# A two-layer recurrent and windowed-attention kernel: the second feed-forward product from rounded parts and rests, one convolution tap on ScalarE

## What is computed

```python
def _layer(x, wqkv, qs, ksc, wo, lg, lb, w1, b1, w2, b2):
    h = shift_token(x)
    ...                                  # q, k, v, rotary, local attention
    x = x + o @ wo
    h = shift_token(x)
    h = (h - mu) / jnp.sqrt(var + 1e-05) * lg + lb
    h = h @ w1 + b1
    a, g = jnp.split(h, 2, axis=-1)
    h = a * jax.nn.gelu(g, approximate=False)
    x = x + h @ w2 + b2
...
x_conv = _causal_depthwise_conv(x, conv_w, conv_b)   # four taps
r_t = jax.nn.sigmoid(x_conv @ W_r.T + b_r)
i_t = jax.nn.sigmoid(x_conv @ W_i.T + b_i)
a_t = a_base ** (8.0 * r_t)
inp = i_t * x_conv                       # then a scan over the tokens
```

## Time and profile before

| | |
|---|---|
| median of 3 runs | 1350.91 us (1349.66 to 1351.91) |
| profiled execution | 1352.94 us, span of its instructions 1351.1 us |
| mean granted TensorE clock | 0.987 of full speed |
| TensorE busy | 1274.2 us (94%) |
| ScalarE busy | 1105.8 us (82%) |
| VectorE busy | 1104.1 us (82%) |
| GpSimd busy | 1009.0 us (75%) |

### The profile page before, as it was taken

One profiled execution on the slowest core, in us unless ns is written; L12 is line 12 of the kernel. 1 busy time (PEld: TensorE's weight loads), 2 busy tenths in 40 slices (PEclk: granted clock), 3 DMA queues, 4 the chain that ended last, 5 costly groups with the idle time before them and its releaser, 6 DMA issues.

```text
span 1351.1 us, 37630 instructions
## 1 busy us (share of the span) xinstructions
PE 1274.2 (94%) x13656; PEld 996.8 (74%) x13656; DVE 1104.1 (82%) x1929; ACT 1105.8 (82%) x3413; POOL 1009.0 (75%) x744
## 2 busy tenths in 40 slices
PE   3898999999999999999988999999999999999997
PEld 2687888888888887655547888888878888876664
DVE  2888888888888888577768899999899999974887
ACT  2688999999999898554448999999999999997654
POOL 4798999999999987212139999999999999982110
PEclk8899999999999999999999999999999999999999
DMA  5222222222223221011011121111221111110222
GB/s 155 52 60 60 60 65 64 61 61 68 60 60 75 56 50 37 17 33 29 0 26 37 45 52 46 45 44 45 52 53 45 45 45 45 41 33 24 78 75 82
DMA packets 60600, 70.33 MB, mean 52 GB/s; under 512 B 8961, under 2 KB 38529, under 8 KB 60417
## 3 DMA queue, kind: packets, MB, share of 16 engines
q1 hardware_dynamic: 60416, 67.93, 20.1%
HBM read 13.40 MB, written 4.19 MB: 13 GB/s over the span
## 4 chain that ended last, share of the span: by engine, by line
PE 83%; ACT 5%; issue 4%; DVE 3%; DMA 2%; POOL 2%; SPq 1%; ACTq 0%; DVEq 0%; POOLq 0%
PE ps L172 66%; PE ps L231 9%; PE ps L241 4%; PE ps L244 4%; ACT P L580 2%; DMA norm<-X 1%; DVE t L817 1%; POOL t L1070 1%; DVE t L826 1%; ACT Vn L594 0%; PE ps L391 0%; PE ps L177 0%; DMA hsh<-X 0%; DVE sums L833 0%; POOL side L1101 0%
## 5 line engine op out<-in xcount | busy, mean ns | idle before, releaser
L580 ACT ACTIVATE P<-ps,nm 128x128 f32<-128x128 f32 x1024 | 364.0, 384 | 0.0
L172 PE MATMUL ps<-wqkv,hT 128*128 128x512 f32 x1152 | 334.0, 433 | 15.4 <-DVE t L817 8.8
L1070 POOL TENSOR_TENSOR t<-t 128x1024 f32<-128x1024 f32 x128 | 306.2, 2392 | 37.7 <-DVE t L817 36.1
L1070 POOL TENSOR_TENSOR P<-P,rden 128x512 f32<-128x512 f32 x256 | 296.9, 1166 | 48.4 <-DVE rden L852 45.9
L172 PEld LDWEIGHTS ps<-wqkv,hT 128*128 128x128 f32 x1152 | 219.4, 192 | 92.3 <-issue 35.9
L1070 POOL TENSOR_TENSOR t<-t,rr 128x1024 f32<-128x1024 f32 x128 | 243.8, 1905 | 16.6 <-ACT rr L563 16.5
L580 ACT ACTIVATION_READ_ACCUMULATOR P<-ps,nm 128x1 f32 x1024 | 230.0, 225 | 0.0
L826 DVE TENSOR_TENSOR t<-ps,tabl 128x512 f32<-128x512 f32 x256 | 164.2, 683 | 41.3 <-ACT sqk L554 40.5
L1070 POOL TENSOR_TENSOR hnr<-B,hnr 128x512 fp32r<-128x512 f32 x32 | 41.8, 1307 | 195.0 <-ACT hnr L618 195.0
L570 ACT ACTIVATE PT<-ps 128x1024 f32<-128x1024 f32 x128 | 130.6, 1020 | 65.8 <-PE ps L231 64.8
L845 DVE TENSOR_REDUCE nm<-ps 128x4 f32<-128x512 f32 x256 | 173.8, 681 | 4.2 <-PE ps L172 4.2
(11 more groups left out here) (117 smaller groups left out, 2423.3 us busy)
## 6 DMA issues: line engine op xcount, KB each, us to landing
Vs<-Vn SPq DMA_DIRECT2D x224, 128.0 KB, 2.3
side<-in_x SPq DMA_DIRECT2D x16, 256.0 KB, 3.0
hsh<-X SPq DMA_DIRECT2D x32, 128.0 KB, 2.2
A<-X SPq DMA_DIRECT2D x16, 256.0 KB, 2.5
norm<-X SPq DMA_DIRECT2D x32, 128.0 KB, 2.3
oT<-in_x SPq DMA_DIRECT2D x16, 256.0 KB, 3.0
out<-oT SPq DMA_DIRECT2D x16, 256.0 KB, 2.2
hsh<-X SPq DMA_DIRECT2D x32, 127.8 KB, 2.3
```

The source lines that it names most:

```text
L172: return e.matmul(o, lhsT, rhs, start=start, stop=stop, skip_group_check=True)
L580: k = act(P[:, g, :], ps[:, 3 + s, (g % 4) * 128:(g % 4 + 1) * 128], ACT.Exp, bias=nm[:, g:g + 1], accum_out=den[:, g:g + 1])
L1070: return e.tensor_tensor(o, a, b_, op)
```

## The change

1. **Second feed-forward product.** `w2` is split once per layer into a rounded part and a rest (`w2r`), at `i == 5` on ScalarE and `i == 6` on VectorE. Each chunk of `hxf` is split by ScalarE (copy into the rounded part) and GpSimd (subtraction), new functions `split_hx`, into the double-buffered `hxr`; `hxf` itself has a single buffer now, so `hidden(b, j)` waits until GpSimd has read chunk `j` of the block before. `down` makes nine `float32r` products.
2. **Newest convolution tap.** The first of the four taps of `conv`, with the bias, is one ScalarE activation with scale and bias from columns; VectorE makes the other three after it.
3. **1/128.** `avg` is a column broadcast to 128x128 in place of a matrix loaded from memory.
4. **Places.** `w2` lands in a part of `norm` that `h2` uses later, `room` moves, and SP no longer waits for `s_y` ahead of loading layer 1's `w2`.

```diff
-        w2 = sb("w2", [128, 3, 128])
+        w2r = sb("w2r", [128, 2, 3, 128], F32R)
-        avg = sb("avg", [128, 128])
...
+        avg = part.to_broadcast([128, 128])
...
             def down(l, b):
                 m = l * NB + b
                 if b == 0:
-                    e.wait_ge(s_w2, 16 * (l + 1))
+                    e.wait_ge(s_w2lo, l + 1)
                 if b:
                     e.wait_ge(s_xf, m)
                 for j, (o, n) in enumerate(CH):
-                    e.wait_ge(s_hxf, 3 * m + j + 1)
-                    k = mm(ps[:, 6, :], w2[0:n, j, :], hxf[0:n, b % 2, j, :], j == 0, j == 2)
+                    e.wait_ge(s_hxhi, 3 * m + j + 1)
+                    mm(ps[:, 6, :], w2r[0:n, 1, j, :], hxr[0:n, b % 2, 0, j, :], j == 0, False)
+                    mm(ps[:, 6, :], w2r[0:n, 0, j, :], hxr[0:n, b % 2, 0, j, :], False, False)
+                for j, (o, n) in enumerate(CH):
+                    e.wait_ge(s_hxlo, 3 * m + j + 1)
+                    k = mm(ps[:, 6, :], w2r[0:n, 0, j, :], hxr[0:n, b % 2, 1, j, :], False, j == 2)
                 k.then_inc(s_y, 1)
...
+            def split_hx(l, b, j):
+                m, n = l * NB + b, CH[j][1]
+                e.wait_ge(s_hxf, 3 * m + j + 1)
+                if b == 0:
+                    e.wait_ge(s_av, (l + 1) * NT)
+                elif b > 1:
+                    e.wait_ge(s_y, m - 1)
+                act(hxr[0:n, b % 2, 0, j, :], hxf[0:n, j, :], ACT.Copy).then_inc(s_hxhi, 1)
+
+            def conv(b):
+                if b > 1:
+                    e.wait_ge(s_xi, b - 1)
+                act(cv[b % 2], seq(A, b), ACT.Identity, scale=cw[3], bias=CB).then_inc(s_cv0, 1)
...
                     if b < NB:
-                        for j in range(3):
-                            gelu(l, b, j)
+                        gelu(l, b, 0)
+                        gelu(l, b, 1)
+                        split_hx(l, b, 0)
+                        gelu(l, b, 2)
+                        split_hx(l, b, 1)
+                        if l:
+                            split_hx(l, b, 2)
...
+                        split_hx(l, b, 2)
+                        if b + 1 < NB:
+                            conv(b + 1)
                         gates2(b)
...
-                if b > 1:
-                    e.wait_ge(s_y, m - 1)
-                e.scalar_tensor_tensor(hxf[0:n, b % 2, j, :], ps[0:n, j, :], b1g[0:n, 0, j:j + 1], gl[j][0:n, :],
+                if m % NB:
+                    e.wait_ge(s_hxlo, 3 * (m - 1) + j + 1)
+                e.scalar_tensor_tensor(hxf[0:n, j, :], ps[0:n, j, :], b1g[0:n, 0, j:j + 1], gl[j][0:n, :],
                                        ALU.add, ALU.mult).then_inc(s_hxf, 1)
...
             def conv(b):
                 x, y = seq(A, b), cv[b % 2]
-                if b > 1:
-                    e.wait_ge(s_xi, b - 1)
-                ts(y, x, cw[3], CB, ALU.mult, ALU.add).then_inc(s_cv, 1)
                 for q, j in enumerate((2, 1, 0)):
-                    e.wait_ge(s_cv, 4 * b + q + 1)
+                    if q:
+                        e.wait_ge(s_cv, 3 * b + q)
+                    else:
+                        e.wait_ge(s_cv0, b + 1)
                     e.scalar_tensor_tensor(y[:, 3 - j:], x[:, :L - 3 + j], cw[j], y[:, 3 - j:], ALU.mult, ALU.add).then_inc(s_cv, 1)
...
+            def split_hx(l, b, j):
+                m, n = l * NB + b, CH[j][1]
+                e.wait_ge(s_hxhi, 3 * m + j + 1)
+                tt(hxr[0:n, b % 2, 1, j, :], hxf[0:n, j, :], hxr[0:n, b % 2, 0, j, :].bitcast(F32),
+                   ALU.subtract).then_inc(s_hxlo, 1)
```

More of the change, by code:

```diff
@@ L85, in program @@
         with ExitStack() as phase:
-            sp_("kept", [128, 2048])
+            room = sp_("room", [128, L])
+            sp_("kept", [128, 2048 - L])
             hnr = sp_("hnr", [128, 2, 2, L], F32R)
-            hxf = sp_("hxf", [128, 2, 3, L])
-            room = sp_("room", [128, L])
+            hxf = sp_("hxf", [128, 3, L])
+            hxr = sp_("hxr", [128, 2, 2, 3, L], F32R)
         CB, BR, BI, LA = (cols[:, i:i + 1] for i in range(4))
         cw = [cols[:, 4 + j:5 + j] for j in range(4)]
-        one, eps_ln, eps_rms, ln2x8, mln2 = (cst[:, i:i + 1] for i in range(5))
+        one, eps_ln, eps_rms, ln2x8, mln2, part = (cst[:, i:i + 1] for i in range(6))
+        avg = part.to_broadcast([128, 128])
         ax, ez, u, dd, lnu, ru, half, nx, mx = (ab[:, i:i + 1] for i in range(9))
@@ L108, in program @@
         w1 = norm[:, L:L + 2 * HID]
+        w2 = norm[:, 128:L].rearrange("p (j d) -> p j d", j=3)
         xe = [oT[:, 0, :], oT[:, 1, :]]
@@ L164, in program @@
             sem(n_) for n_ in ("s_hxf", "s_xf", "s_cv", "s_xi", "s_a2n", "s_hs", "s_osum", "s_eg", "s_em", "s_eo"))
-        s_zero, s_nmr, s_nrm, s_add, s_tn, s_pn, s_hi, s_h, s_hnlo, s_a2, s_in = (
-            sem(n_) for n_ in ("s_zero", "s_nmr", "s_nrm", "s_add", "s_tn", "s_pn", "s_hi", "s_h", "s_hnlo", "s_a2", "s_in"))
+        s_zero, s_nmr, s_nrm, s_add, s_tn, s_pn, s_hi, s_h, s_hnlo, s_a2, s_in, s_hxlo = (
+            sem(n_) for n_ in ("s_zero", "s_nmr", "s_nrm", "s_add", "s_tn", "s_pn", "s_hi", "s_h", "s_hnlo", "s_a2", "s_in", "s_hxlo"))
         def tensor(e):
@@ L442, in tensor @@
                         if l == 0 and b == 0:
-                            e.wait_ge(s_wts, 48)
+                            e.wait_ge(s_wts, 32)
                             e.wait_ge(s_x, 3)
@@ L702, in scalar @@
                         act(w1r[:, 0, :], w1, ACT.Copy, scale=lcol(l, 0)).then_inc(s_whi, 1)
+                    if i == 5:
+                        e.wait_ge(s_w2, 16 * (l + 1))
+                        if l:
+                            e.wait_ge(s_y, NB)
+                        act(w2r[:, 0, :, :], w2, ACT.Copy).then_inc(s_w2hi, 1)
                     if i == NT + 1:
@@ L709, in scalar @@
                         exps(l, i - 2, 0)
+                    if l == 0 and i == NT + 1:
+                        e.wait_ge(s_tx, NB)
+                        conv(0)
                     if l == 0 and i == 9:
@@ L816, in rotate @@
                         e.wait_ge(s_tpk, n - 1)
+                    if n == NT:
+                        e.wait_ge(s_hxf, 3 * NB)
                     e.tensor_tensor(o1, qk, C, ALU.mult).then_inc(s_t2, 1)
@@ L957, in end_out @@
                 e.tensor_tensor(g, g, xe[b % 2], ALU.add).then_inc(s_eo, 1)
-            for i, v in enumerate((1.0, LN_EPS, RMS_EPS, 8 * LN2, -LN2)):
+            for i, v in enumerate((1.0, LN_EPS, RMS_EPS, 8 * LN2, -LN2, 1.0 / D)):
                 e.memset(cst[:, i:i + 1], v)
@@ L1031, in vector @@
                                                ALU.mult, ALU.subtract).then_inc(s_wlo, 1)
-                    if l == 0 and i == NT:
-                        e.wait_ge(s_tx, NB)
+                    if i == 6:
+                        e.wait_ge(s_w2hi, l + 1)
+                        e.tensor_tensor(w2r[:, 1, :, :], w2, w2r[:, 0, :, :].bitcast(F32), ALU.subtract).then_inc(s_w2lo, 1)
+                    if l == 0 and i == NT + 2:
                         conv(0)
@@ L1181, in gpsimd @@
                         split_hn(l, b + 1)
+                    if b < NB:
+                        for j in range(3):
+                            split_hx(l, b, j)
                     if l == 0 and b == 9:
@@ L1202, in load_w2 @@
             def load_w2(l):
-                e.dma_start(w2[:], d["w2"][:, l]).then_inc(s_w2, 16)
+                e.dma_start(w2, d["w2"][:, l]).then_inc(s_w2, 16)
             def shift_rows(o, x, landed):
@@ L1254, in sync @@
                 e.dma_start(t_[:], d[n]).then_inc(s_mask, 16)
-            for t_, n in ((avg, "avg"), (wo, "wo"), (wr, "wr")):
+            for t_, n in ((wo, "wo"), (wr, "wr")):
                 e.dma_start(t_[:], d[n]).then_inc(s_wts, 16)
@@ L1286, in sync @@
                     load_w1(1)
-                    e.wait_ge(s_y, NB)
                     load_w2(1)
@@ L1370 @@
         "x": a["x"], "cols": cols, "idf": eye, "idb": eye.astype(ml_dtypes.bfloat16),
-        "mask": mask.astype(ml_dtypes.bfloat16), "avg": np.full((128, 128), 1.0 / D, np.float32), "tab": tab,
+        "mask": mask.astype(ml_dtypes.bfloat16), "tab": tab,
         "wr": np.stack([a["W_r"].T, a["W_i"].T, a["W_out"].T], 1),
```

15 lines of the change are left out of this document (8 added, 7 removed).

## The result

| | median | lowest to highest | runs | ratio, 95% interval |
|---|---|---|---|---|
| before | 1350.29 us | 1348.72 to 1351.91 | 4 | |
| changed | 1388.76 us | 1383.96 to 1391.27 | 4 | 1.0281, 1.025 to 1.0311 |

The change makes the kernel slower by 2.8%, 38.5 us; 1384 was forecast, and the range was 1360 to 1398. The profiled execution took 1388.31 us (span 1386.5), 35.4 us more span than before, where 33.5 had been summed; between the medians it is 38.5.

What follows compares the result with a forecast made beforehand. Circles of waits among in-order queues, with VectorE-GpSimd collisions, were to bound the feed-forward blocks instead of TensorE: 18.3 + 14.5 + 0.7 = 33.5 us on 1352.94 gives 1386.4, median 1384 us; range 1360 to 1398.

Steps and rivals of the forecast that it cites:

- TensorE's part: Feed-forward blocks: nine rounded down products save 0.48 us; if nothing else binds, blocks take 7.98 and 6.72 us.
- Rival 3: Feed-forward stages: the circle stays open, TensorE's saving of 15 us shows, 1336 us; chance 0.07.
- The durations: Single operations: ScalarE tap 0.80 us, GpSimd subtraction 1.29, copy 0.62; a collided VectorE operation ends 0.55 after GpSimd's.
- Layer 0's circle: Layer 0's feed-forward: engines wait in a ring with two tap collisions; block 9.6 us for 8.46, +18.3 us with extras.
- The two collisions: Layer 0 block: tap 1 under a hidden-feature subtraction, tap 2 under the hnr one, each ending 0.55 us after it.
- Layer 1's circle: Layer 1's feed-forward: the end_out product collides with the hnr subtraction; block 8.35 us for 7.20, +14.5 us.
- rival 2: Both feed-forward stages: one collision a block drops out, blocks 8.67 and 7.42 us, total 1361 us; chance 0.12.
- extras: Layer 0: copy, wqkv split, table products and shifts, formerly hidden under TensorE, join the circle: 4.6 us, bounds 2 and 5.7.
- blocks 0 to 3 are held as before: Layer 0's first blocks: table loads and the last layer norm hold them, so only twelve blocks grow, 13.7 us.
- rivals 1: Both feed-forward circles with their collisions as summed, 1384 us, own range 1371 to 1396; chance 0.71.
- Rival 4: Longer: tap 3 is hit too (1397 us), or TensorE's waits of about 1.7 us a block lower its clock; chance 0.10.
- The rest: Attention in both layers: +0.7 us, bounds 0 and 4; the broadcast column and the dropped DMA: nothing.

Runs made afterwards that it cites:

- experiment 9: Changed kernel with ScalarE reordered, layer 0's rest subtractions shared between GpSimd and VectorE, and first and last blocks' order mended: 1346.36 us, 0.9967 of before.
- experiment 6: Changed kernel with ScalarE's queue reordered in both layers, every operation kept: 1360.07 us, 1.0058 of before.
- experiment 1: Changed kernel with hxf in two buffers again: 1389.84 us (1 run).
- 3: Changed kernel with GpSimd's hxr subtractions cut to two columns, leaving out the rest of the hidden features: 1383.93 us (1 run).
- 4: Changed kernel with the newest tap back on VectorE and GpSimd's hxr subtractions cut to two columns: 1364.69 us (1 run).
- experiment 5: Changed kernel with layer 1's split of h moved on ScalarE from the front to behind gelu 1: 1379.18 us (1 run).
- the second run of experiment 7: Kernel before with only the newest convolution tap and its bias moved to ScalarE: 1352.0 us, 1.0009 of before.
- experiment 7: Kernel before with one part of the change at a time: broadcast column only, 1351.55 us; newest tap on ScalarE only, 1352.0 us.

## Why the prediction was right, point by point

**TensorE's part.** `down` is nine records, and the blocks that nothing else binds take 7.99 and 6.69 to 6.72, for the 7.98 and 6.72 of the step. Rival 3 gave that state 1336 us; experiment 9 came near it in the steady blocks (8.05 and 6.69), not at the edges. TensorE was to be busy 83% and 80%: its work is 84% and 82% of a block (7.98 of 9.45, 6.72 of 8.22), while the windows say 89%: TensorE's rows cover 8.4 of the 9.45 us, more than that work.

**The durations.** The tap on ScalarE is 0.806 for 0.80, the subtraction 1.287 for 1.29, the copy 0.63 for 0.62, the collision's end 0.55 after the release, as in the earlier trace rows.

**Layer 0's circle.** In the prediction's count, from `hidden(b,0)` at 663.88: GpSimd's subtractions 1.49 to 5.24 (1.54 to 5.34 predicted), tap on ScalarE at 3.49 (3.58), taps from 4.33 (4.42), tap 1 to 5.79 (5.89), the `hnr` subtraction to 6.94 (7.04), tap 2 to 7.49 (7.59), the next `hidden` at 9.45 (9.6). The two collisions are the two that were named, with taps of 1.46 and 1.66 us. That another order of the same work opens the circle is shown by experiment 6; that the buffer isn't part of it, by 1; that the subtractions are, by 3 and 4.

**Layer 1's circle.** 8.22 for 8.35, with the product of `end_out` hit at the median (1.68) as before, and 1.0 us less once it isn't (experiment 5; rival 2 had put 7.42 on this, 7.22 was measured).

**The sizes that were off.** Layer 0: 18.3 was 13.7 for twelve blocks and 4.6 for extras; measured are 19.6, of which 10.9 is eleven blocks of 0.99, 4.6 the extras, and 4.0 lie in blocks 0 to 3, which had been taken as unchanged. There the prediction's step, that blocks 0 to 3 are held as before, was wrong. Block 0 takes 2.7 more. In 1.5 of it TensorE waits for the first tanh (2.63 us for 1.16 before), ahead of which ScalarE now has two copies and a wait for `hidden`; 1.1 stands with the tap alone too (the second run of experiment 7: 13.64 for 12.52, and there attention 0 is 1.2 shorter). Layer 1: 14.5 had come from thirteen blocks; measured are 16.3, but differently made up. Counted by `up`, only eight blocks reach 8.22 (8.1 us); blocks 1 and 3 to 6 take 1.0 less in sum, because TensorE runs ahead of the circle, and what follows the last `up` takes 5.8 more, in which that is paid back. Counted from one `hidden(b,0)` to the next, eleven steps, from block 3 on, take 8.22 for 7.20: thirteen of 1.15 were forecast (15.0), eleven of 1.02 are 11.2. And the block with the last layer norm takes 12.85 for 9.44. The timeline of the changed kernel there, TensorE and ScalarE, behind two rows of TensorE in block 0 of layer 0:

```profile
556.17 1.70 PE L175 MATMUL ps<-side,wr 128*128 128x512 f32 x2 [2.63 <-ACT B L654]
556.88 6.19 PE L175 MATMUL ps<-hnr,w1r 128*128 128x512 f32 x18
...
1266.85 1.08 PE L398 MATMUL ps<-idf,X 128*128 128x128 f32 x4 [4.42 <-ACT norm L542]
1267.58 5.51 PE L175 MATMUL ps<-hnr,w1r 128*128 128x512 f32 x18
...
1262.90 0.63 ACT L643 ACTIVATE hxr<-hxf 85x512 fp32r<-85x512 f32 x1 [0.35 <-DVE hxf L967]
1263.44 1.26 ACT L536 ACTIVATE A<-A,ro 128x128 f32<-128x128 f32 x4
1264.72 1.28 ACT L778 ACT_TABLE_LOAD   x1
1266.02 0.69 ACT L542 ACTIVATE norm<-ps,cst 128x512 f32<-128x512 f32 x1
```

TensorE waits 4.42 us for the norm, 0.87 before: three copies and the waits for `hidden` that come with them stand ahead of table load and norm. The prediction had no term for it. The order counts here too: the first three blocks of layer 1 take 30.0 us in the changed kernel, 27.1 before, and 27.2 in experiment 6, where the norm stands ahead of the third copy and `rec_scale`.

That the total came so near (35.4 for 33.5) is in part luck. In each layer too many growing blocks were counted and the first blocks were left out, and these errors have opposite signs; and attention 0 happened to take 2.4 less in the profiled execution. The medians differ by 38.5, which is 5 more than was summed. The chances of rivals 1, 2 and 4 add up to 0.93, not 0.92.

**The rest.** +0.7 was put on attention; +1.5 in attention 1 and 0.4 in the tail were measured, the rest of attention is scatter (experiment 1). The tap and the column alone change nothing that can be told apart in the time (experiment 7).

**The two rules that bear on this.** The Trainium skill ("SBUF — State Buffer", Who interferes with whom) calls the port pair that VectorE and GpSimd share an exclusive lock, and says of VectorE's modes with two ports that the one that comes second fully blocks. The trace agrees that the second waits for the first to end; that it then takes 0.55 us more, and not its full 0.75 or 0.69, is what the trace adds, and the earlier trace rows decided rightly. The Trainium skill ("Perfetto Trace Analysis", Identifying the Most-Contended Engine) has the engine of highest occupancy optimised first, but wants TensorE's headroom judged by its weight loads and not by its matmuls' busy time. Here the weight loads were busy 74%, ScalarE and VectorE 82%, so by that measure TensorE was not first, and the change put 58 us on ScalarE. The 0.48 us a block that TensorE saves shows once nothing else binds (experiments 4 and 9).

**Rival 4's clock** is seen in the rows, but costs little. The last two short windows above have a granted clock of 0.51 and 0.50 of full speed, the lower of TensorE's two levels, 1.2 GHz; the one from 555 to 560, 0.66, lies partly at it. The stretch in layer 1 follows 4.42 us without work (to 1266.85), and the `up` behind it takes 5.51 us for 4.75; the one in block 0 follows 2.63 us (`up` takes 6.19 there). The regular wait of 1.03 us a block lowers nothing: the window from 640 to 690 has 1.00. What it costs in layer 0 can be read from experiment 1, whose feed-forward stage had the full clock throughout, though TensorE waited as long (2.64 us) in block 0 there. Its window:

```profile
545.10:716.20 171.10, 145.01 (x564) 93.44 (x561) 123.16 (x147) 111.88 (x188) 91.51 (x72) 1.00 0.06 17
```

Its blocks 0 to 3 take 45.7 us in sum, as in the changed kernel, and its blocks 4 and 5 take 21.0, as there: where the circle binds, a slower TensorE is hidden. The stage is 1.3 us shorter (171.1 for 172.4), all of it behind the last `up`, where a `down` takes 2.36 us for 3.68. The kernel before had a stretch at the lower level there too (0.72 from 691 to 697), so in layer 0 the clock is no part of the difference. In layer 1 it is at most the 0.8 us of that `up` and some 0.5 of the transposes ahead of it; no run parts that.
